# Four attention and feed-forward layers in one program: first steps of a stage run at the end of the stage before

## The reference

```python
# pair 0: softmax attention over [context; x];  feed-forward with int8 activations and ternary weights, gelu-like gate
x = x + L0_xattn(layernorm(x), context);   x = x + L0_ffn(layernorm(x))
x = x + L1_xattn(layernorm(x), context)
# feed-forward two (pair 1)
def L1_ffn(x):                                     # x: tokens x 512, weights 2048 x 512
    inter = silu(bitlinear(x, w_gate)) * bitlinear(x, w_up)
    return bitlinear(fwht(inter), w_down)          # fwht: normalized Walsh-Hadamard transform over 2048
def bitlinear(v, w):   return act_quant(v) @ weight_quant(w).T
def act_quant(v):      # per token: scale = 128 / max|v|; round, clip to [-128, 127], divide by scale
def weight_quant(w):   # round(w / mean|w|) clipped to -1, 0, 1, times mean|w|
# third attention (pair 2), linear attention
q    = feature(x @ Wq.T);  gate = sigmoid(x @ Wg.T + bg)   # feature(v) = v + 1 if v > 0 else exp(v)
attn = (q @ kv_summary) / (q . k_sum + 1e-6)               # summaries over the context, per head of 32
x = x + (attn * gate) @ Wo.T
```

## Time and profile before

| | us |
|---|---|
| median of 3 runs (2162.09 to 2168.79) | 2167.9 |
| profiled execution, device time | 2166.01 |
| its span, first to last instruction | 2164.2 |
| TensorE matmul busy | 2036.5 (94%) |
| VectorE busy | 1152.8 (53%) |
| ScalarE busy | 825.2 (38%) |
| GpSimd busy | 182.0 (8%) |
| mean granted TensorE clock | 0.979 |

### The profile page before, as it was taken

One profiled execution on the slowest core, in us unless ns is written; L12 is line 12 of the kernel. 1 busy time (PEld: TensorE's weight loads), 2 busy tenths in 40 slices (PEclk: granted clock), 3 DMA queues, 4 the chain that ended last, 5 costly groups with the idle time before them and its releaser, 6 DMA issues.

```text
span 2164.2 us, 28614 instructions
## 1 busy us (share of the span) xinstructions
PE 2036.5 (94%) x10533; PEld 1156.7 (53%) x10556; DVE 1152.8 (53%) x2597; ACT 825.2 (38%) x1717; POOL 182.0 (8%) x466
## 2 busy tenths in 40 slices
PE   8999999999999798999999999999689888888999
PEld 3444444444666344555555555466444455556665
DVE  1324455258122485675666666578556568864221
ACT  1333223312111264554544554455332245553331
POOL 1011110000000121110111111011000000000000
PEclk9999999999999999999999999999899989998999
DMA  5355342551641421020000001220000322210000
GB/s 232 134 214 202 154 160 92 211 200 53 211 148 64 150 104 47 22 101 22 24 26 23 22 22 44 92 78 21 19 16 13 134 92 85 91 55 6 11 11 15
DMA packets 60315, 185.12 MB, mean 86 GB/s; under 512 B 10578, under 2 KB 29010, under 8 KB 54463
## 3 DMA queue, kind: packets, MB, share of 16 engines
q1 hardware_dynamic: 58451, 145.55, 19.5%
q0 software_dynamic: 1728, 37.75, 4.5%
HBM read 124.61 MB, written 49.50 MB: 80 GB/s over the span
## 4 chain that ended last, share of the span: by engine, by line
PE 82%; DVE 12%; ACT 3%; issue 2%; DMA 1%; SPq 1%; POOL 0%; DVEq 0%; ACTq 0%
PE psum L120 58%; PE psum L113 8%; PE psum L1567 5%; PE psum L2594 5%; PE psum L1611 5%; DVE small L2473 2%; PE psum L1155 1%; PE psum L2402 1%; DVE R L1322 1%; DVE R L1321 1%; DVE WK L2479 1%; DMA R<-in_wkv 1%; DVE small L301 1%; DVE WK L324 1%; DVE WK L1312 0%
## 5 line engine op out<-in xcount | busy, mean ns | idle before, releaser
L120 PE MATMUL psum<-R,WK 128*125 128x512 f32 (+11 forms) x3080 | 1047.0, 486 | 30.9 <-DMA WK<-in_ctxT 7.5
L120 PEld LDWEIGHTS psum<-R,WK 128*112 128x112 f32 (+4 forms) x3094 | 504.1, 171 | 521.2 <-issue 407.8
L113 PE MATMUL psum<-small,WK 112*125 112x112 f32 (+5 forms) x2036 | 280.1, 268 | 65.9 <-DVE WK L1312 20.0
L113 PEld LDWEIGHTS psum<-small,WK 112*125 112x125 f32 (+5 forms) x2036 | 225.6, 155 | 171.7 <-issue 83.7
L120 PE MATMUL psum<-WK,R 128*32 128x128 f32 (+3 forms) x1752 | 201.3, 358 | 4.3 <-ACT WK L2433 1.9
L120 PE MATMUL psum<-R 128*128 128x112 f32 (+4 forms) x832 | 146.8, 326 | 10.5 <-DVE R L1928 9.3
L120 PEld LDWEIGHTS psum<-WK,R 128*32 128x32 f32 (+3 forms) x1752 | 109.7, 137 | 68.4 <-issue 20.7
L120 PEld LDWEIGHTS psum<-R 128*128 128x128 f32 (+2 forms) x832 | 102.8, 182 | 56.5 <-issue 41.4
L1661 ACT ACTIVATE WK<-psum,small 112x487 f32<-112x487 f32 x128 | 96.9, 757 | 76.7 <-DVE small L1746 72.7
L1567 PE MATMUL psum<-R,WK 128*112 128x512 f32 x256 | 120.1, 592 | 0.0
L1743 DVE TENSOR_TENSOR psum<-psum,R 112x112 f32<-112x112 f32 x128 | 35.1, 274 | 152.8 <-PE psum L120 152.8
(11 more groups left out here) (238 smaller groups left out, 2155.8 us busy)
## 6 DMA issues: line engine op xcount, KB each, us to landing
R<-in_wf POOLq DMA_DIRECT2D x6, 4096.0 KB, 13.7
d_w<-R POOLq DMA_DIRECT2D x6, 2048.0 KB, 19.5
R<-d_w SPq DMA_DIRECT2D x6, 2048.0 KB, 10.5
WK<-in_ctxT SPq DMA_DIRECT2D x16, 750.0 KB, 6.6
d_v<-WK SPq DMA_DIRECT2D x16, 750.0 KB
R<-in_wq SPq DMA_DIRECT2D x7, 1024.0 KB, 8.3
R<-in_wo SPq DMA_DIRECT2D x6, 1024.0 KB, 15.8
d_k<-X SPq DMA_DIRECT2D x8, 750.0 KB, 5.2
```

The lines of the kernel that those rows point to most:

```text
L113: ins = pe.transpose(dst, src, idn[0:k, 0:k])
L120: ins = pe.matmul(dst, lhs, rhs, start=k == 0, stop=k == len(pairs) - 1)
```

## The change

It has five parts.

- In the context part, the fourth Abs stands on ScalarE behind the drain of `T_2` instead of behind that of `k3_3`.
- The statistics and the normalization of att0's batch 0 (`first`) stand on VectorE at the end of the context part, ahead of the copies of its last `kv_0`. The buffers `xnT`, `qT` and `kT` of att0 lie 1024 columns further on.
- SP issues the loads of ffn0's tiles 0 and 1 ahead of the coefficient stores of the last two batches of att0.
- In ffn1, VectorE quantizes tile 1 ahead of the gating of tile 0; the two instructions that make the small signed matrix (L1287, L1288) stand behind it, and TensorE waits for them in iteration 2 instead of 1.
- In ffn1's last tile, all four first levels `w0` to `w3` stand ahead of the transposes of the tile before. att2's batch 0 is begun in ffn1's last two iterations: normalization in the one, `xnT`, q, g, the exponential, the feature and the bias in the other. Two psum lists are written anew for it, so `w2`, `w3` and the `hi` banks come in another order in all tiles (the bank of `hi0` is that of `w0` of the same iteration).

```diff
@@ -574,7 +574,8 @@
                                 act.wait_ge(sem("k3_stored"), 16 * b)
                             ins = act.activation(k3o[:, j, :], src[:, 0:S], ACT.Identity, bias=bk3[:, j:j + 1])
                         ins.then_inc(act_ring.sem_drained, 1)
-                        if kind == "k3" and b < 6:
+                        j = dict(k3_0=0, k3_1=1, k3_2=2).get(name, 3 if name == f"T_{NS - 1}" else None)
+                        if j is not None and b < 6:
                             if j == 0:
                                 act.wait_ge(sem("context_raw"), 16 * (b + 1))
                                 if b:
@@ -582,6 +583,7 @@
                             act.activation(tern[:, j * 2048:(j + 1) * 2048], raw[:, j * 2048:(j + 1) * 2048], ACT.Abs,
                                            accum_out=wsum[:, b, j:j + 1]).then_inc(sem("context_abs"), 1)
                         if kind == "v2":
+                            j = int(name[-1])
                             act.wait_ge(sem("context_low"), NS * b + j + 1)
                             if NS * b + j:
...
@@ -631,6 +633,8 @@
                                 coefficients(dve, link, 2)
                             if s == 2:
                                 split_coefficients(dve, link)
+                    if b == NB - 1:
+                        stages[0]["first"](dve)
                     dve_ring.wait_filled(dve, b, "kv_0")
...
-            def sync(sp, load_next):
+            def sync(sp, load_next, load_tiles):
                 context_stored(sp)
...
                     store_coefficients(sp, b - 2)
+                load_tiles(sp, range(2))
                 for b in (NB - 2, NB - 1):
                     store_coefficients(sp, b)
...
-                dve.wait_ge(sem("x_loaded"), 16 * 5)
-                ln_stats(dve, link, n, 0)
                 for b0, b1, b2 in iterations(3):
...
+            def first(dve):
+                dve.wait_ge(sem("x_loaded"), 16 * 5)
+                ln_stats(dve, dve_chain.on(dve), n, 0)
+                ln_apply(dve, n, 0, xn).then_inc(sem(f"{stage}_xn"), 1)
...
                 order = [g for c in range(FC) for g in ((f"h{c}", H), (f"g{c}", G))]
-                order += [(g, H if g[0] == "w" else 3) for g in ("w0", "w1", "hi0", "w2", "hi1", "w3", "hi2", "hi3")]
+                order += [("w0", H), ("w1", H), ("w2", H, [NT - 1]), ("w3", H, [NT - 1]), ("next_xnT", 3, [NT - 1]), ("hi0", 3),
+                          ("-", 3, []), ("w2", H, range(NT - 1)), ("hi1", 3), ("w3", H, range(NT - 1)), ("hi2", 3), ("hi3", 3)]
             else:
+            ahead = [("-", 3, []), ("next_q", 3, [NT - 1]), ("next_g", 3, [NT - 1])] if hadamard else []
             act_ring, dve_ring = rings(stage, range(5), order + [("xiT", Q)],
-                                       range(5, 8), [(f"u{c}", G) for c in range(FC)] + [("y", 3)], tiles=NT)
+                                       range(5, 8), [(f"u{c}", G) for c in range(FC)] + ahead + [("y", 3)], tiles=NT)
...
@@ -1161,19 +1170,24 @@
                         if i == 1:
                             x_ready(pe, n)
                             pe.wait_ge(sem(f"{stage}_weights"), 16 * 3)
+                        if i == 2:
                             pe.wait_ge(sem(f"{stage}_signs"), 1)
                         for c in range(FC):
                             if b2 is not None:
                                 turn_h(b2, c)
                             if b1 is not None:
                                 gate_up(b1, c)
+                        last = b2 == NT - 1
                         for c in range(FC):
                             if b2 is not None:
                                 first_levels(b2, c)
-                            if b3 is not None and c:
+                            if b3 is not None and c and not last:
+                                if c == 1 and b3 == NT - 1:
+                                    stages[n + 1]["head_pe"](pe)
                                 turn_hi(b3, c - 1)
                         if b3 is not None:
-                            turn_hi(b3, FC - 1)
+                            for c in range(FC) if last else [FC - 1]:
+                                turn_hi(b3, c)
                         if b0 is not None:
                             turn_xi(b0)
...
                 if hadamard:
                     for b0, b1, b2, b3 in iterations(4, NT):
+                        last = b2 == NT - 1
+                        if b3 == NT - 1:
+                            stages[n + 1]["head_act"](act)
...
-                            if b3 is not None and c:
+                            if b3 is not None and c and not last:
                                 drain_hi(b3, c - 1)
                         if b3 is not None:
-                            drain_hi(b3, FC - 1)
+                            for c in range(FC) if last else [FC - 1]:
+                                drain_hi(b3, c)
+                            if b3 == NT - 1:
+                                stages[n + 1]["exponentials"](act, 0)
...
-                if hadamard:
-                    dve.wait_ge(sem(f"{stage}_weights"), 16 * 3)
-                    dve.tensor_copy(plus_minus[:, 0, :], had)
-                    dve.tensor_scalar(plus_minus[:, 1, :], had, -1.0, None, ALU.mult).then_inc(sem(f"{stage}_signs"), 1)
-
...
                 if hadamard:
+                    def next_x(b):
+                        quantize_x(dve, b)
+                        if b + 1 < NT:
+                            stats(dve, b + 1)
+
                     for b0, b1, b2, b3 in iterations(4, NT):
+                        if b1 == 0:
+                            next_x(b0)
+                            dve.wait_ge(sem(f"{stage}_weights"), 16 * 3)
+                            dve.tensor_copy(plus_minus[:, 0, :], had)
+                            dve.tensor_scalar(plus_minus[:, 1, :], had, -1.0, None, ALU.mult
+                                              ).then_inc(sem(f"{stage}_signs"), 1)
                         for c in range(FC):
                             if b1 is not None:
                                 if b2 is not None:
                                     act_ring.wait_filled(dve, b2, f"h{c}")
                                 gated(b1, c)
+                        if b3 == NT - 2:
+                            stages[n + 1]["first"](dve)
                         if b3 is not None:
                             quantize_h(b3)
-                        if b0:
-                            quantize_x(dve, b0)
-                            if b0 + 1 < NT:
-                                stats(dve, b0 + 1)
...
-                            if b3 == NT - 1:
-                                stages[n + 1]["first"](dve)
...
+                        if b2 == NT - 1:
+                            stages[n + 1]["head_pool"](pool)
...
+            def exponentials(act, b):
+                act.wait_ge(sem(f"{stage}_low"), b + 1)
+                act.activation(ex, low, ACT.Exp).then_inc(sem(f"{stage}_exp"), 1)
+            def below_zero(dve, b):
+                ring, *use = dve_of(b, "q")
+                ring.wait_filled(dve, *use)
+                dve.tensor_scalar(low, ring.bank[use[1]][0:T, :], 0.0, None, ALU.min).then_inc(sem(f"{stage}_low"), 1)
+            def queries_and_gates(dve, b):
+                ring, *use = dve_of(b, "q")
+                dve.wait_ge(sem(f"{stage}_exp"), b + 1)
+                if b:
+                    act_ring.wait_filled(dve, b - 1, "fqT")
+                dve.scalar_tensor_tensor(fq, ring.bank[use[1]][0:T, :], 0.0, ex, ALU.max, ALU.add
+                                         ).then_inc(ring.sem_drained, 1)
+                ring, *use = dve_of(b, "g")
+                ring.wait_filled(dve, *use)
+                if b:
+                    dve.wait_ge(sem(f"{stage}_gate"), b)
+                else:
+                    dve.wait_ge(sem(f"{stage}_bias"), 16)
+                dve.tensor_tensor(gl, ring.bank[use[1]][0:T, :], bg, ALU.add).then_inc(ring.sem_drained, 1)
+            def head_dve(dve):
+                below_zero(dve, 0)
+                queries_and_gates(dve, 0)
+            def head_pe(pe):
+                pe.wait_ge(sem(f"{stage}_weights"), 48)
+                turn_x(pe, 0)
+                project(pe, 0, "q", wq)
+                project(pe, 0, "g", wg)
+            def head_act(act):
+                turned_x(act, 0)
+            def head_pool(pool):
+                ln_power(pool, pool_chain.on(pool), n, 0)

...
-                    if b1 is not None:
-                        act_ring.wait_drained(pe, b1, "xnT")
-                        dve_ring.wait_free(pe, b1, "q")
-                        product(pe, dve_ring.bank["q"][0:T, :], [(xnT[:, kt, :], wq[:, kt, :]) for kt in range(KT)]
-                                ).then_inc(dve_ring.sem_filled, 1)
+                    if b1:
+                        project(pe, b1, "q", wq)
...
```

(4 more changed lines are left out.)

103 lines of the change are left out of this document (57 added, 46 removed).

## The result

| | before | after |
|---|---|---|
| median of 4 runs each, us | 2168.4 (2162.1 to 2168.9) | 2134.3 (2132.0 to 2135.0) |
| ratio, with its 95% interval | | 0.9848 (0.9828 to 0.9867) |
| span of the profiled execution | 2164.2 | 2130.1 |
| TensorE matmul busy | 2036.5 | 2030.8 |
| mean granted clock | 0.979 | 0.986 |

What follows compares the result with a forecast made beforehand. TensorE, busy 94% of the span, bounds the kernel, so gains come only from its waits and the half clock behind them. The five parts sum to 35.8: 2166.0 becomes 2130.2, with the median 1.9 higher, 2132 us; range 2122 to 2142.

Steps and rivals of the forecast that it cites:

- The sum: Whole kernel: the five places' savings, 10.7 + 0.8 + 8.5 + 4.6 + 11.2, make 35.8 us.
- Part 1: Context part: TensorE's waits for the T_2 and turn drains go; 10.7 us saved, bounds 9.5 and 11.2.
- Part 2: att0's start: transposes 2.5 us earlier, mostly given back waiting for the last store's landing; 0.8 saved, bounds -1.5 and 3.
- Part 3: ffn0's start: the wait for the tile's transfer goes, half clock mostly too; 8.5 us saved, bounds 6 and 9.
- Part 4: ffn1's start: the 3.40 wait and the half clock behind it go; 4.6 us saved, bounds 2.5 and 5.5.
- Part 5: ffn1's end, att2's start: the 10.19 wait is filled, down ends earlier; 11.2 us saved, bounds 8 and 15.
- w3 started where it was put: ffn1's last tile: w3 from 1535.0 at half clock; VectorE's second half 3.9 us earlier, down ending 5.4 earlier.
- from the end of down to the next transposes: att2's start: twelve spline units and one normalization take 7.8 us before batch 1's transposes, 7.3 less than before.
- the first product behind: att2: first q product behind the spline units runs at half clock, 5.33 us against 3.69; 1.5 given back.
- The rival in which the units alone take 9 us: att2, iteration 1: spline units take 9 us instead of 4.6, half clock again; saving there 6, total 2137; chance 0.08.
- Exp as the new end: att2's start: tile 6's update waits behind Exp and bias, 1558.2 against down's 1557.7; 3 us lost, 2135; chance 0.07.
- The rule of the Trainium skill: TensorE clock: any short wait left may or may not bring half clock, some 1.5 us each, five seen; sum unmoved.

Runs made afterwards that it cites:

- The parts alone: Five kernels, each the kernel before with one of the change's five parts, in order: 2152.6, 2168.3, 2155.0, 2166.1, 2157.8 us.
- The stores-first kernel: Changed kernel with stores of values 1 and 3 in the last context batch issued before the fourth key drain's wait and next context-row load: 2130.8 us, ratio 0.9839.
- the repeat: The changed kernel run once more, unaltered, on another chip beside the kernel before: 2133.4 us, ratio 0.9853.
- part 4 alone: Kernel before with only ffn1's tile 1 quantized ahead of tile 0's gating and the signed matrix behind it: 2166.1 us, ratio 1.0000.

## Why the prediction was right

- **The sum.** The parts alone give 10.9 - 0.2 + 9.2 + 5.2 + 10.7 = 35.8 at their places, the forecast's 35.8. That it is the same to the tenth is luck: the parts were off by 0.2 to 1.0 each, both ways, and a place repeats to between 0.4 and 1.5 us from trace to trace. The changed kernel's own trace gives 34.1, since it started 0.7 late and stopped for 1.1 at 402.50. The parts don't overlap: each acts on another stretch. By the medians of their runs the parts alone add up to 29.7 (13.6 - 2.2 + 11.2 + 0.0 + 7.1), the whole change to 34.1 and 31.5.
- **Part 1** (10.7): 10.9. The Abs that was pushed back made no new wait of TensorE. The forecast counted no clock here, since the trace of before shows no fall behind these waits; six other traces do, and the runs gained 13.6.
- **Part 2** (0.8): -0.2 to 1.0 in the five traces that have it and not the earlier stores; those without it give -0.5 to 1.0, so the size can't be told. The reason was right: VectorE waits 16.60 for the landing instead of 14.26, and the third iteration moved by 0.8 to 0.9. The stores-first kernel shows the mechanism by lifting it.
- **Part 3** (8.5): 9.2. The clock stayed up entirely, where I had kept 0.4 of the loss.
- **Part 4** (4.6): 4.9 to 5.2 at its place. As a change of the whole time it isn't shown: by the medians it is 0.0 alone and 0.7 in its absence, by the ratios 0 and 3.5.
- **Part 5** (11.2): 10.3 to 11.9. Three terms were off and nearly cancelled, which is luck. First, w3 started where it was put (1510.95, with the 24.1 saved so far: 1535.0), but ran at full clock, since the fall of the stretch before it didn't come; VectorE's second half started 5.3 earlier instead of 3.9, and down ended 6.8 earlier instead of 5.4. Second, from the end of down to the next transposes I had 7.8, and it is 9.2: I spaced the units as in the first seven and one transposition, but of twelve in a row the later ones wait up to 1.8, and the normalization took 1.36 beside GpSimd's writes instead of 0.55. Third, the first product behind took 5.86 where I took 5.33, and 4.34 in the repeat, where the half-clock stretch at that spot is 6.8 us long and not 10.2; that is the 1.5 between 10.3 and 11.9. The rival in which the units alone take 9 us was right on the duration, though it put the part at 6.
- **Exp as the new end**, a rival: true for the last update, by as little as its own sum said (1558.2 against 1557.7). L335 starts when the bias behind Exp is done, 0.5 later than down alone would let it; the first unit's copy behind it came 0.2 later against the first unit than before (1533.66 - 1532.10 against 1564.37 - 1562.98), and TensorE waits neither for Exp nor for the update. Nothing like the 3 us of the rival was lost.
- **Clock.** The rule of the Trainium skill ("TensorE: Matmul & The Clock Gate", Part 1), that the monitor runs free, had been left outside the sum. The traces agree with it: the same wait of 1.8 us ahead of the same product at 76 us is followed by full clock in the kernel before and by 3.4 us at half clock with part 4 alone, two kernels whose code is the same up to there.
